# A macaron layer on one core: the feed-forward's stages between the MLP's matmuls, set one slot later and packed into fewer slots

## The reference

```
def small_ffn(x):                        # 512 -> 64 -> (64 x 16) -> 64 -> 512
    s = x @ Win + bin_                   # 64 values a token
    h = relu(s[..., None] * W1 + b1)     # 16 relu pieces for each of them
    g = sum(h * W2, -1) + b2
    return g @ Wout + bout

def attn(x):                             # x is LN of the stream
    y = delta_rule_attention(rmsnorm(x, ln1)) + x     # 16 heads, a state of 32 x 32 each
    return gelu(rmsnorm(y, ln2) @ w1 + b1) @ w2 + b2 + y    # 512 -> 2048 -> 512

x = x + 0.5 * small_ffn(LN(x))
x = x + attn(LN(x))
x = x + 0.5 * small_ffn(LN(x))
```

## Time and profile before

| | before |
|---|---|
| median of 3 runs | 3310.32 us |
| lowest, highest run | 3310.03, 3311.62 us |
| the profiled execution's own time | 3311.62 us |
| its span in the profile | 3309.8 us |
| PE busy | 3179.2 us, 96% |
| DVE busy | 1841.6 us, 56% |
| ACT busy | 1308.4 us, 40% |
| POOL busy | 1205.1 us, 36% |
| mean granted TensorE clock | 0.982 |

### The profile page before, as it was taken

The page is one execution under the profiler, slowest core; times in us unless marked ns, Lnnn a source line. Parts: engine busy times, 40 slices in busy tenths (PEclk is TensorE's granted clock), DMA queues, the critical chain, the costliest instruction groups (busy, mean ns, idle before and its releaser), DMA issues.

```text
span 3309.8 us, 150288 instructions
## 1 busy us (share of the span) xinstructions
PE 3179.2 (96%) x68438; PEld 2594.1 (78%) x68438; DVE 1841.6 (56%) x2965; ACT 1308.4 (40%) x2654; POOL 1205.1 (36%) x1211
## 2 busy tenths in 40 slices
PE   5999999999958999999999999999999999999998
PEld 4777777777747888898888778887777888777886
DVE  6787878778648899888323333233333323333324
ACT  5444445444313333333343333333333433333333
POOL 1435564655526776666211222211222212122211
PEclk8999999999969999999999999999999999999999
DMA  3445555455465677666661110101110110111010
GB/s 111 144 148 167 141 162 154 145 152 162 139 201 181 220 227 228 215 197 207 200 184 35 39 39 13 39 26 39 39 39 17 36 39 26 39 39 38 14 39 26
DMA packets 388865, 356.00 MB, mean 108 GB/s; under 512 B 58256, under 2 KB 321680, under 8 KB 385680
## 3 DMA queue, kind: packets, MB, share of 16 engines
q1 hardware_dynamic: 386400, 351.86, 34.2%
q10 hardware_dynamic: 2224, 0.90, 0.2%
HBM read 184.65 MB, written 153.09 MB: 102 GB/s over the span
## 4 chain that ended last, share of the span: by engine, by line
PE 65%; DMA 2%; SPq 0%; DVE 0%; issue 0%; ACT 0%; DVEq 0%; ACTq 0%
PE bank L237 14%; PE bank L235 14%; PE bank L236 14%; PE bank L1238 13%; PE bank L1283 5%; PE bank L1698 2%; PE bank L1689 2%; DMA ringB<-heads_scratch 1%; PE bank L1681 1%; PE bank L1672 1%; DMA Z<-z_scratch 0%; DVE g L2010 0%; PE bank L1745 0%; SPq L1147 0%; ACT relu L1867 0%
## 5 line engine op out<-in xcount | busy, mean ns | idle before, releaser
L1939 DVE TENSOR_TENSOR glo<-gl,gh 128x512 fp32r<-128x512 f32 x256 | 196.0, 766 | 823.5 <-ACT gh L1817 821.8
L1813 ACT ACTIVATE gl<-bank,b1m 128x512 f32<-128x512 f32 x256 | 176.0, 687 | 736.4 <-PE bank L237 730.9
L235 PE MATMUL bank<-h,w_hi 128*128 128x512 f32 x1024 | 421.1, 411 | 0.1
L235 PE MATMUL bank<-w_hi,gh 128*128 128x512 f32 x1024 | 402.7, 393 | 0.9 <-DVE glo L1939 0.9
L237 PE MATMUL bank<-h,w_lo 128*128 128x512 f32 x1024 | 401.3, 392 | 0.0
L237 PE MATMUL bank<-w_hi,glo 128*128 128x512 f32 x1024 | 400.5, 391 | 0.0
L236 PE MATMUL bank<-h,w_hi 128*128 128x512 f32 x1024 | 399.4, 390 | 0.0
L236 PE MATMUL bank<-w_lo,gh 128*128 128x512 f32 x1024 | 399.2, 390 | 0.0
L236 PEld LDWEIGHTS bank<-h,w_hi 128*128 128x128 f32 x1024 | 193.4, 189 | 49.2 <-issue 10.7
L235 PEld LDWEIGHTS bank<-h,w_hi 128*128 128x128 f32 x1024 | 192.5, 188 | 48.7 <-issue 10.8
L1238 PE MATMUL bank<-ringA 32*32 32x32 f32 x16512 | 221.9, 196 | 5.3 <-issue 4.3
(11 more groups left out here) (200 smaller groups left out, 7086.1 us busy)
## 6 DMA issues: line engine op xcount, KB each, us to landing
ringB<-heads_scratch SPq DMA_DIRECT2D x257, 192.0 KB, 3.3
ringA<-heads_scratch SPq DMA_DIRECT2D x260, 128.0 KB, 2.8
X<-in_L_attn_x SPq DMA_DIRECT2D x16, 1024.0 KB, 10.1
x_scratch<-X SPq DMA_DIRECT2D x16, 1024.0 KB, 4.5
heads_scratch<-vb SPq DMA_DIRECT2D x16, 1024.0 KB, 5.2
heads_scratch<-qk SPq DMA_DIRECT2D x16, 1024.0 KB, 6.6
heads_scratch<-kb SPq DMA_DIRECT2D x16, 1024.0 KB, 5.2
heads_scratch<-kbuf SPq DMA_DIRECT2D x16, 1024.0 KB, 7.2
```

Source lines behind the costliest of these rows:

```text
L235: e.matmul(o, lhs[0], rhs[0], start=first, stop=False)
L1813: e.activation(gl[k][:, :], bank[1 - k][:, :], ACT.Gelu_apprx_tanh, bias=b1m[:, m:m + 1]).then_inc(a_gl, 1)
L1939: e.tensor_tensor(gh[k][1][:, :], gl[k][:, :], gh[k][0][:, :], ALU.subtract).then_inc(v_gl, 1)
```

## The change

Three functions `ffn(t, m)` of the dense part, those of PE, ACT and DVE, get other slot numbers. Nothing else changes: the same instructions are issued with the same operands and waits.

| stage | slots before | slots after |
|---|---|---|
| `stats` of 4 blocks, `mean` (DVE) | 0 | two blocks in 0, two and `mean` in 1 |
| `shift` (DVE) | 1 | 2 |
| `normalize` (ACT) | 1, 2 | 2, 3 |
| `turn_x` (PE), `x_turned` (ACT) | 3, 4 | 4, 5 |
| `hidden` (PE) | 5 | 6 |
| relus (ACT) and sums (DVE) | 2 in 5, 3 in 6, 3 in 7 | 4 in 6, 4 in 7 |
| `ffn_out` (PE), `add_ffn` (DVE) | 8, 9 | 8, 9 |

```
             def ffn(t, m):                                # PE
-                if m in (3, 4):
-                    turn_x(t, 2 * (m - 3))
-                    turn_x(t, 2 * (m - 3) + 1)
-                elif m == 5:
+                if m in (4, 5):
+                    turn_x(t, 2 * (m - 4))
+                    turn_x(t, 2 * (m - 4) + 1)
+                elif m == 6:
                     hidden(t)
...
             def ffn(t, m):                                # ACT
-                if m == 1:
+                if m == 2:
                     normalize(t, 0)
                     normalize(t, 1)
-                elif m == 2:
+                elif m == 3:
                     normalize(t, 2)
                     normalize(t, 3)
-                elif m in (3, 4):
-                    x_turned(t, 2 * (m - 3))
-                    x_turned(t, 2 * (m - 3) + 1)
-                elif m == 5:
-                    relus(t, 0, 1)
+                elif m in (4, 5):
+                    x_turned(t, 2 * (m - 4))
+                    x_turned(t, 2 * (m - 4) + 1)
                 elif m == 6:
-                    relus(t, 2, 3, 4)
+                    relus(t, 0, 1, 2, 3)
                 elif m == 7:
-                    relus(t, 5, 6, 7)
+                    relus(t, 4, 5, 6, 7)
...
             def ffn(t, m):                                # DVE
                 if m == 0:
-                    for b in range(NB):
-                        stats(t, b)
+                    stats(t, 0)
+                    stats(t, 1)
+                elif m == 1:
+                    stats(t, 2)
+                    stats(t, 3)
                     mean(t)
-                elif m == 1:
+                elif m == 2:
                     shift(t)
-                elif m == 5:
-                    sums(t, 0, 1)
                 elif m == 6:
-                    sums(t, 2, 3, 4)
+                    sums(t, 0, 1, 2, 3)
                 elif m == 7:
-                    sums(t, 5, 6, 7)
+                    sums(t, 4, 5, 6, 7)
```

## The result

| | before | after |
|---|---|---|
| median | 3310.92 us (4 runs) | 3336.18 us (4 runs) |
| lowest, highest | 3310.03, 3311.62 | 3334.51, 3337.94 |
| the profiled execution's span | 3309.8 us | 3335.3 us |
| PE busy in the span | 3179.2 us | 3188.6 us |

The ratio is 1.0081, with a 95% interval of 1.0067 to 1.0094: the change makes the kernel slower by 25 us. 3334.3 us was forecast. The ratios in this document are taken over the compared runs and are not the quotient of the two medians, from which they differ by up to 0.0008.

What follows compares the result with a forecast made beforehand. PE was taken to bound the dense part. A loss of 1.6 us a tile in 15 tiles, 24 us, on the profiled 3311.62 us gave 3335.6, less 1.3 for the median: 3334.3 us, range 3319 to 3346.

Steps and rivals of the forecast that it cites:

- PE bounds the dense part: From 1800 to 3280 us PE is busy 1479.11 of 1480.00 us, so at most 0.9 us could be gained.
- What moves without a price: Statistics through hidden layer, loads and POOL's additions go one slot later as a group, at a cost of nothing.
- Five slow and four free instructions on DVE: Of nine sums and remainder per tile, five keep POOL's 1.71 us pitch; four after its last addition run at free length.
- the old clock: Times counted with relu 0 kept at 2243.84, as in the kernel before, and deadlines set one 5.46 us slot earlier.
- First deadline: PE's `down` needs the remainder glo of slot 7, wanted at 2251.88; PE starts it at 2252.92, losing 1.04 us.
- Second deadline: PE's `ffn_out` needs the last sum, due 2254.60: 1.51 us late including the first pause, 1.61 with the restart.
- The clock stays at 1.00: PE's new pauses, about 0.9 and 0.3 us a tile, leave the granted clock in the dense part at 1.00.
- The rival that gave it 0.04: Much slower: PE's pauses also lower the clock, 1.8 us more a tile, 3361 us in all; chance 0.04.
- The rival "no change": The chain still fits: all sums take 0.75 us, PE does not wait, time 3310.3 us; chance 0.10.
- The bounds: DVE's chain: no loss if all free, 80 us if all slow; one turn fewer or more, 3320 or 3349 us.
- The pitch of 1.71: While POOL adds, DVE does one instruction for each addition of POOL, one every 1.71 us.
- the first part's row with 0.91: In the first part, 3.6 us without PE work gave a granted clock of 0.91 over 20 us, 1.8 us lost.

Runs made afterwards that it cites:

- the whole chain one slot later: The changed kernel, but relus and sums in groups of two, three and three in slots 6 to 8, ffn_out and add_ffn in 9 and 10: ratio 1.0001.
- the remainder ahead of sum 3: The changed kernel, but on DVE the remainder of slot 7 comes before sum 3, not after it: 3338.58 us, ratio 1.0079.
- the additions from sum 1 on: The changed kernel, but POOL's eight additions of a tile wait until sum 1 is done: 3399.58 us, ratio 1.0266.
- additions behind the last sum: The changed kernel, but POOL's eight additions of a tile wait until the last sum is done: 3312.70 us, ratio 0.9998.

## Why the prediction was right

The forecast was 3334.3 us (3319 to 3346), and 3336.18 us were measured. Step by step:

- *PE bounds the dense part, so a pause is paid in full and nothing can be gained.* Right. The tile grew by 1.62 us and 15 of them are 24.3 of the span's 25.5 us. On average over the tiles it is 1.7 us, which is the whole. Of the seven experiments, none is faster than before beyond its interval.
- *What moves without a price.* Right, shown by the whole chain one slot later. POOL's additions kept their place relative to the first relu, as assumed (3.32 us ahead, 3.31 before).
- *Five slow and four free instructions on DVE.* Right, and by number: set back to the old clock (2255.58 for 2243.84), the remainder of slot 7 ends at 2252.83, forecast 2252.86, and sum 7 at 2256.07, forecast 2256.05. The two kernels with POOL's additions moved show that it is POOL, in both directions.
- *First deadline, 1.04 us late.* Measured 1.02 us.
- *Second deadline, about 0.4 us more, and no sum of two losses.* Measured 0.33 us, and the experiment with the remainder ahead of sum 3 shows that removing the first pause gains nothing. The whole lateness at `ffn_out` was forecast at 1.51 us. In the old clock it started at 2267.86 - 11.74 = 2256.12, due at 2254.60, so 1.52 us late, and with the restart (0.11) that is the 1.6 of the sum. The restart behind the first pause costs 0.18 us, not 0.10, which doesn't touch the sum, since DVE does not wait for PE in this chain.
- *The clock stays at 1.00.* Right in the changed kernel. The rival that gave it 0.04 was wrong only about the size of the pause: at 3.7 us it came true.
- *The rival "no change"* had a wrong detail. Its own terms, eight relus at 0.77 us and 1.3 for the gelu, fill ACT to 2251.3 in the old clock, not to 2251.7. So its last sum would end at about 2252.1, not at 2252.5. With POOL's additions out of the way, the first relu started at 2152.04 and the last sum ended at 2160.36, which makes 2252.2.
- *The bounds* use 0.93 and 0.95 us for what one turn beside POOL adds. The pitch of 1.71 less 0.75 is 0.96. This changes neither end of the range by a full us.
- In an expectation, not in the prediction, I left out the clock for a pause of 3.9 us (the additions from sum 1 on), though the first part's row with 0.91 had shown its size, 1.8 us. At 1.9 us a tile, 28 us in all, that was nearly the whole miss of 30 us.

## What to carry to other kernels

When one engine is busy all the time, read from the timeline when it asks for what the other engines make, and how long before that each is ready. That reserve, not the busy share of those engines, decides what packing their work costs. Work of POOL beside it can double the length of DVE's instructions, so the length must be taken from rows with the same neighbour. And of several late deliveries of one chain that does not itself wait for the busy engine, only the last counts in full: taking away an earlier wait can gain nothing. A busy share near 100% doesn't show that nothing is late, either: compare the number of instructions done in the same stretch.

## What the runs showed of the hardware

- DVE and POOL took turns, one instruction for one, where the DVE instruction had both inputs in SBUF: 0.75 us grew to 1.6 to 1.8 for a sum of 128x512, and POOL's 1.27 us to 1.62 to 1.75. Sum 0, with one tensor input in SBUF, grew too, from 0.55 to 1.37 us. A remainder that started 0.20 us ahead of POOL's addition kept its 0.69 us, and POOL's took 1.63 us (additions behind the last sum, at 2161.66 us). An addition of DVE with one input in PSUM (0.69 us) was not slowed by POOL's, nor POOL's by it.
- A matmul that waited for DVE started 0.05 to 0.06 us after DVE's instruction ended and took 0.11 us more than usual (0.50 for 0.39), and the eleven behind it 0.07 us more in all.
- TensorE's clock: pauses of 1.0 and 0.3 us in otherwise full work left the granted clock at 1.00 (2.4 GHz). One of 3.7 us a tile brought it to 0.50 (1.2 GHz) for a few us, at 1.9 us a time on average, and one of 6.9 us cost hardly more, 2.1 us.
